# All warm-up matmuls on TensorE left out of an eight-layer transformer-like network

## The reference

```
x += tanh(g) * gat(ctx features, adjacency from layernorm(x))  # graph attention: 2 layers, 8 heads of 32
x += tanh(g) * moe(rms attention(x))                           # 16 heads of 16, rope; 8 experts, 2 chosen, and a shared one
x += latent_attention(layernorm(x), ctx)                       # 16 heads, compressed keys and values
x += low_rank(layernorm(x))                                    # base matrix and 64 rank-one terms, 8 chosen
x += score_attention(...)                                      # 1 head of 64, with a mask
x += tokens chosen by a router with a capacity through a small feed-forward part
x += small_attention(layernorm(x));  x += moe(layernorm(x))
```

## Time and profile before

| | |
|---|---|
| median of 3 runs | 1481.78 us |
| lowest and highest | 1475.41 and 1498.99 us |
| span of the profiled execution, first to last instruction | 1470.0 us |
| instructions in it | 20110 |
| granted clock, mean over the span | 0.875 |
| busy: PE, PEld, DVE, ACT, POOL | 1177.5, 991.0, 890.3, 634.7, 229.2 us |

### The profile page before, as it was taken

The page is one execution under the profiler, slowest core; times in us unless marked ns, Lnnn a source line. Parts: engine busy times, 40 slices in busy tenths (PEclk is TensorE's granted clock), DMA queues, the critical chain, the costliest instruction groups (busy, mean ns, idle before and its releaser), DMA issues. The chain is left out here.

```text
span 1470.0 us, 20110 instructions
## 1 busy us (share of the span) xinstructions
PE 1177.5 (80%) x7232; PEld 991.0 (67%) x7232; DVE 890.3 (61%) x2074; ACT 634.7 (43%) x1166; POOL 229.2 (16%) x256
## 2 busy tenths in 40 slices
PE   6968869899799723986998978984289979679797
PEld 4556748678589623764786867983267868568676
DVE  3366867377576455765755765746456557556465
ACT  3355727344254213673653424421056434447242
POOL 0000032034100000000402420000034034231132
PEclk9999889789899955897987999996589889899799
DMA  9100000122000000000002300000020032200131
GB/s 373 50 8 1 1 1 1 37 87 92 1 1 1 5 0 10 1 1 1 1 1 88 101 26 1 2 1 4 20 60 1 1 101 76 80 0 1 58 93 54
DMA packets 19458, 52.89 MB, mean 36 GB/s; under 512 B 3360, under 2 KB 5664, under 8 KB 19232
## 3 DMA queue, kind: packets, MB, share of 16 engines
q1 hardware_dynamic: 19360, 51.58, 10.7%
HBM read 50.52 MB, written 1.05 MB: 35 GB/s over the span
## 5 line engine op out<-in xcount | busy, mean ns | idle before, releaser
L1032 POOL TENSOR_TENSOR p_WML<-p_raw,p_WMH 128x768 fp32r<-128x768 f32 (+1 forms) x78 | 136.6, 1757 | 222.6 <-ACT p_WMH L1103 222.6
L209 PE MATMUL PS<-onesb,identb 128*128 128x512 bf16 x312 | 104.5, 482 | 81.8 <-PEq L175 67.5
L1233 DVE TENSOR_TENSOR p_ALO<-p_A,p_AHI 128x512 fp32r<-128x512 f32 x78 | 117.6, 1507 | 78.8 <-ACT p_AHI L1148 78.7
L196 POOL TENSOR_SCALAR rstd<-mv 128x4 f32<-128x4 f32 x18 | 4.5, 251 | 798.8 <-DVE mv L192 321.3
L90 PE MATMUL PS<-HH,p_WMH 128*128 128x512 f32 x280 | 116.7, 417 | 4.6 <-DVE p_A L1229 2.6
L209 PEld LDWEIGHTS PS<-onesb,identb 128*128 128x128 bf16 x312 | 34.0, 119 | 125.9 <-issue 94.9
L91 PE MATMUL PS<-HL,p_WMH 128*128 128x512 f32 x280 | 114.3, 408 | 0.0
L92 PE MATMUL PS<-HH,p_WML 128*128 128x512 f32 x280 | 113.9, 407 | 0.0
L818 PEld LDWEIGHTS PS<-p_V,p_PTS 128*128 128x128 f32 x768 | 97.9, 205 | 0.0
L818 PE MATMUL PS<-p_V,p_PTS 128*128 128x17 f32 x768 | 96.7, 266 | 0.0
L1103 ACT ACTIVATE p_WMH<-p_raw 128x896 fp32r<-128x896 f32 (+1 forms) x78 | 69.9, 907 | 56.8 <-PE PS L92 56.0
(11 more groups left out here) (334 smaller groups left out, 3230.7 us busy)
## 6 DMA issues: line engine op xcount, KB each, us to landing
p_raw<-in_moe SPq DMA_DIRECT2D x62, 448.0 KB, 3.3
p_fr<-in_fold SPq DMA_DIRECT2D x16, 512.0 KB, 7.8
p_raw<-in_ffn SPq DMA_DIRECT2D x16, 320.0 KB, 3.1
p_raw<-in_wpack SPq DMA_DIRECT2D x7, 512.0 KB, 8.1
CP<-in_consts SPq DMA_DIRECT2D x1, 1720.0 KB, 12.9
XALL<-in_x SPq DMA_DIRECT2D x1, 1024.0 KB, 16.0
p_ctr<-in_ctxT SPq DMA_DIRECT2D x4, 256.0 KB, 3.0
out<-XALL SPq DMA_DIRECT2D x1, 1024.0 KB, 4.5
```

The source lines that it names most:

```text
L209: pe.matmul(PS[:, bank, :], identb[:, :], onesb[:, :].unsqueeze(1).broadcast_to([P, 4, P]), start=True, stop=True)
L1032: g.tensor_tensor(WML[:, i % RING, :], raw[:, i % RAW, 0:SEL], WMH[:, i % RING, 0:SEL].bitcast(F32), ALU.subtract).then_inc(s["w_lo"], 1)
L1233: v.tensor_tensor(ALO[:, i % 3, :], A[:, b, :], AHI[:, i % 3, :].bitcast(F32), ALU.subtract).then_inc(s["a_lo"], 1)
```

## The change

The five counts become 0, so that no call of `warm` issues anything. All waits and all other instructions stay, in their order. The constants identb and onesb are still made.

```diff
 WARM = {
-    "rms": 12,
-    "norm": 4,
-    "split": 8,
-    "weights": 4,
-    "elu": 4,
+    "rms": 0,
+    "norm": 0,
+    "split": 0,
+    "weights": 0,
+    "elu": 0,
 }
```

## The result

The changed kernel takes 1522.7 us (median of 4 runs, 1519.8 to 1525.8) against 1482.6 us (median of 4, 1475.4 to 1499.0): ratio 1.026, 95% interval 1.019 to 1.033. It is slower beyond doubt; that it is so by more than 2% is likely and not certain, since the interval begins at 1.9%. Forecast were 1524 us, +2.8%.

The account below looks back on a forecast made before the run. DVE was taken to pace the graph loops, PE's clock to be paid in full in other loops and hidden tiles. Terms summed to +42 us on the timed median of 1481.78: 1524 us, +2.8%, range 1506 to 1544.

Parts of the forecast that it names:

- the loops' term: Four graph-attention loops: at 0.50 PE's step exceeds DVE's 4.0 us; +18.5 us, after 1 us off each loop.
- the third rival: Graph loops at 0.50 throughout, their delay also meeting ACT and DVE, rises at 5.7 us: 1546 us, chance 0.10.
- The clock in the graph loops: Graph loops: short matmuls don't hold the clock, so it stays 0.50 for most of their length; PE's step 4.98 us.
- The first rival: Graph loops keep 1.00 because PE works in every step, giving back some 8 us: 1497 us, chance 0.24.
- Layer 1's prologue: Graph attention, before layer 1's loop: small matmuls, transposes and feature matmuls run at 0.50; twice, +8.0 us (0 to 9).
- Small_attention(0): Start of small_attention(0), twice: slower transposes, and wide work starting at 0.50; +5.7 us (3.9 to 7.3).
- experts(0): Start of experts(0), twice: norm burst's delay given back, mostly covered by POOL's work and DMA data; -1.0 us (-3.8 to +0.4).
- latent: Start of latent_attention, twice: norm burst's 1.25 us given back, wide work starting at 0.50 costs 2.1; +1.7 us (0 to 3.4).
- low_rank: Start of low_rank, twice: 24 matmuls just behind the split burst run partly at 0.50; +3.0 us (0 to 4.2).
- experts(3): Start of experts(3), twice: norm burst's 1.5 us given back, short matmuls and hidden tiles slower; +3.6 us (0 to 6).
- experts(2) and small_attention(3): Starts of both phases, twice each: norm burst's 1.5 us given back, wide work at 0.50 costs 2.1; +2.4 us (-1.8 to +5.2).
- The additive sum: Whole kernel: the terms for graph loops, prologue and phase starts simply add up to +42 us.

Follow-up runs that it names:

- experiment 3: Kernel before with each graph-loop burst made of sixteen 128x16 matmuls in place of four of 128x512: one run, 1500.3 us.
- experiment 4: Changed kernel with the weighted sums of two heads in four left out of the graph loop, a constant instead: one run, 1494.5 us.
- experiments 1: Kernel before with only the graph-loop bursts left out: 1496.6 us, ratio 1.010 (1.002 to 1.018).
- experiment 5: Kernel before with only the norm bursts left out, split bursts kept: 1468.9 us (10 runs), ratio 0.994 (0.990 to 0.998).
- experiment 2: Changed kernel with only the graph-loop bursts of four matmuls a step put back: 1504.4 us, ratio to the kernel before 1.014 (1.005 to 1.024).
- experiment 10: Kernel before without the norm bursts of experts(0), latent_attention and experts(2), the other norm bursts kept: 1472.6 us (12 runs), ratio 0.997 (0.993 to 1.000).
- experiment 9: Kernel before without the elu and split bursts of graph attention, everything else kept: one run, 1485.1 us.

## Why the prediction was right

1524 us were forecast and 1522.7 measured, slower as said, by 2.6% where 2.8% were forecast. The mechanism and the main place of the loss were right. That the number is right to 1 us is luck: the terms were read from profiled spans, and between these the loss is 54 us, 12 more than the 42 forecast, most of it in the loops' term. The medians, to which the 42 were added, differ by only 40, since the profiled run of before was a short one and that of after the longest of four. The loss of 36.9 us in the profiled graph phases lies between the forecast's 26.5 (18.5 + 8.0) and what the third rival had there, 44.5 (22.5 + 8.0 + 14), and two of the things that it named, the clock at 0.50 nearly throughout and a wait for ACT, are in the trace.

- **The clock in the graph loops** (the term that carried the verdict). Rows 6 to 8 were read rightly: the loops run at 0.50, the step is 4.97 to 5.04 us against 4.98 forecast. With PE busy for 16.98 of 17.00 us experiment 3 still has 0.51, and experiment 4 shows that the clock costs because PE's step then exceeds DVE's. The first rival, the loops at 1.00 because PE works in every step, is out by the windows of the changed kernel and of experiments 1 and 3. The Trainium skill ("TensorE: Matmul & The Clock Gate", Part 1) says that activity releases the throttle; read as busy time, this trace disagrees: 25.95 of 26.00 us busy at 0.50.
- **The size of the loops' term**, 18.5, was too small. From the first transposes to the end of L508 the four loops grew by 8.9, 9.0, 4.3 and 9.0 us, 31.1, of which 3.2 came back behind them. Three things: I let the second transposes start where the burst had started, but their numerators come 1.6 us later (the wait of 2.37 us for L607 above); I took 1 us off each loop for a clock that comes back after L496, and it came back in one loop of four (the third, 621.0 to 624.4 in the trace); and the last transposes wait for ACT as well, so that the last step is 5.56 us.
- **Layer 1's prologue**, 8.0: from the end of L508 to the next first transposes, 22.1 us where it was 17.6, twice +4.5, 9.0. Right.
- **Small_attention(0)**, 5.7: 7.6. The products begin 0.74 us later behind the transposes' start (224.35 - 220.16 against 202.23 - 198.78) and run at 0.50 for 4.1 us, +2.0, both as forecast. In the first pair the other 1.2 us stand at the phase's end, where the clock is at 0.50 for 17.1 us (293.3 to 310.4) in place of 13.6 (270.1 to 283.7); the sum had no term for that.
- **experts(0)**, -1.0: -3.4. I held the delay to be covered by POOL's 6 us and the data's arrival. It wasn't: without the norm burst the phase is 2.5 us shorter (experiment 5), and at its products 0.6 us of the 1.25 at the transposes are left, so the chain of transposes and router was on the path. The rest comes behind them, with a shorter stretch at 0.50, and was in no term.
- **latent**, +1.7: +1.6. **low_rank**, +3.0: +1.8. **experts(3)**, +3.6: +3.2. **experts(2) and small_attention(3)**, +2.4: +5.3; the start of the wide work at 0.50 was priced rightly by the hidden tiles, the norm burst gave back about 1.2 us in place of 1.5.
- **The additive sum**: norm bursts alone -8.7 us by the ratio, split and rms bursts alone +29, the loop's alone +15. They sum to 35, the whole is 39 by its ratio; the two elu bursts are in none of the three. So the parts add up about as well as they can be measured, with 6 to 12 us to either side of each.

Left open: why runs of one kernel differ by 2% and more. The kernel before had runs from 1459.8 to 1502.7 us over all series. The two graph phases of one execution, the same instructions, differed by 17 us (experiment 2) where they differ by 3 in the kernel before, and phases that were not touched moved by 1 to 2 us (experiment 10). The traces show what the graph phases' share of this is made of. A loop with its bursts of four mostly takes 36.5 us, with 5.0 to 5.6 us from its second to its third transposes, or 39.2 to 39.6 us, with 8.56 us in most cases for that step, which is all of its work at 0.50. The kernel before has one loop of the long kind, its third, where 1.00 came 15 us after the loop's start and not 6; the kernel of experiment 9 has three, the first, second and fourth. This fits a clock whose rises and falls depend on where the work falls in time, but no run here controlled that alone.

## What to carry to other kernels

A burst of wide matmuls in PE's idle time is worth what its clock does to PE's step behind it: compare the step at 0.50 with the step of the engine that sets the pace, and where the slow step still fits under it the burst is worth nothing. Put the burst where PE waits anyway (behind the transposes here), not ahead of work that is ready soon: those ahead of the transposes cost 9 us in all in experiment 5 (3 to 14), though the other versions without them gained less or nothing. Judge such a change by many runs: the same instructions of a graph loop took 3 us more or less from one profiled kernel to the next (experiments 5, 9 and 10), which is as much as the effects of single bursts.

## What the runs showed that was not expected

- PE without a gap for 26.0 us (25.95 busy) at 0.50, and for 17.0 us (16.98 busy), with sixteen short matmuls more in each step, at 0.51 in the mean.
- The same instruction list in one execution took 134.9 and 117.8 us in its two passes (experiment 2); where they differ, the first has its clock at 0.50 and the second at 1.00.
- Sixteen bf16 matmuls of 128x16 took 0.46 us at 0.50 (118.46 to 118.92), 29 ns each, where f32 ones of 128x8 took 214 ns each at the same clock (24 in 5.14 us) and 113 at 1.00 (24 in 2.70 us, from 1186.13 to 1188.83 in the kernel before).
